# A graph network kernel: inverse roots of the last node updates by GpSimd's pow, and both passes without their last step

## The reference, cut to what matters

```python
h = relu(layernorm(x))
hn = mlp_node(h); he = mlp_edge(edge_attr)                      # 64 wide
msgs = mlp_msg(concat(hn[dst], hn[src], he))                    # 200,000 x 64
agg = segment_sum(msgs, dst) / max(counts, 1)
o = h + mlp_upd(concat(h, agg))
x = x + layernorm(o) * ln_g + ln_b                              # layer 1

h = relu(layernorm(x))
hw = h @ W                                                      # 4 heads of 32
e = leaky_relu(a_src[src] + a_dst[dst])                         # with a loop per node
p = exp(e - segment_max(e, dst))
x = x + segment_sum(hw[src] * p, dst) / segment_sum(p, dst) + bias   # layer 2
```

## Time and profile before

| | us |
|---|---|
| median of 3 runs | 4091.20 |
| lowest and highest | 4089.45, 4092.23 |
| the profiled execution, its own time | 4091.22 |
| its span, from the first to the last instruction | 4089.1 |
| busy: PE, DVE, ACT, POOL | 3382.9, 2517.0, 2850.5, 2965.8 |
| mean granted clock of TensorE | 0.838 of full speed |

### The profile page before, as it was taken

The page is one execution under the profiler, slowest core; times in us unless marked ns, Lnnn a source line. Parts: engine busy times, 40 slices in busy tenths (PEclk is TensorE's granted clock), DMA queues, the critical chain, the costliest instruction groups (busy, mean ns, idle before and its releaser), DMA issues. The chain is left out here.

```text
span 4089.1 us, 126775 instructions
## 1 busy us (share of the span) xinstructions
PE 3382.9 (83%) x30848; PEld 2976.2 (73%) x30849; DVE 2517.0 (62%) x10511; ACT 2850.5 (70%) x5940; POOL 2965.8 (73%) x3134
## 2 busy tenths in 40 slices
PE   7789888999988899999947777777777778777777
PEld 4677777777777788888847777777777767766776
DVE  5752222222222256777748777777777777888888
ACT  6466565656556577788738777777777777877777
POOL 2677777777777777777737777777777777777774
PEclk8789999999899899999967777777777777777777
DMA  5322222222222233333342222222222222332332
GB/s 159 88 60 53 54 55 53 56 53 53 55 54 53 60 83 91 91 96 95 81 120 58 57 58 58 57 58 58 58 57 58 58 58 63 79 78 76 78 78 58
DMA packets 319769, 282.90 MB, mean 69 GB/s; under 512 B 143418, under 2 KB 242924, under 8 KB 319532
## 3 DMA queue, kind: packets, MB, share of 16 engines
q0 software_dynamic: 99456, 159.33, 15.9%
q1 hardware_dynamic: 139224, 79.62, 7.4%
q10 hardware_dynamic: 80852, 41.75, 3.5%
HBM read 249.58 MB, written 29.40 MB: 68 GB/s over the span
## 5 line engine op out<-in xcount | busy, mean ns | idle before, releaser
L541 POOL DMA_INDIRECT a_G<-Htab,idx x1554 | 1470.8, 946 | 526.3 <-issue 464.0
L541 POOL DMA_INDIRECT p_rows<-Btab,idx x1554 | 1471.4, 947 | 475.1 <-issue 473.4
L1799 PE MATMUL a_psA<-a_GP,a_S 128*128 128x132 f32 x4704 | 892.5, 365 | 2.7 <-DVE a_GP L1634 2.7
L1799 PEld LDWEIGHTS a_psA<-a_GP,a_S 128*128 128x128 f32 x4704 | 821.5, 268 | 8.2 <-DVE a_GP L1634 3.1
L1056 DVE TENSOR_TENSOR p_z<-p_psZ,p_rows 128x512 f32<-128x512 f32 x294 | 195.9, 689 | 829.4 <-SPq L746 679.6
L1206 ACT COPY p_ST<-p_psT 128x1024 bf16<-128x1024 bf16 x294 | 300.5, 1022 | 563.7 <-PE p_psT L1318 543.4
L1730 ACT CAST a_S<-a_Sb 128x512 f32<-128x512 bf16 x588 | 608.6, 1144 | 0.0
L1365 PE MATMUL p_psA<-p_msg,p_S 128*128 128x65 f32 x4704 | 589.9, 284 | 10.9 <-ACT p_S L1227 9.8
L1365 PEld LDWEIGHTS p_psA<-p_msg,p_S 128*128 128x128 f32 x4704 | 571.6, 201 | 16.5 <-issue 12.8
L1227 ACT CAST p_S<-p_Sb 128x1024 f32 (+1 forms) x294 | 582.6, 1982 | 0.0
L1341 PEld LDWEIGHTS p_psZ<-wc,p_s 128*128 128x128 f32 x2352 | 325.1, 206 | 204.7 <-issue 103.5
(11 more groups left out here) (212 smaller groups left out, 5165.8 us busy)
## 6 DMA issues: line engine op xcount, KB each, us to landing
arena<-in_ea SPq DMA_DIRECT2D x196, 256.0 KB
p_single<-Btab SPq DMA_DIRECT2D x1792, 0.2 KB
a_single<-Htab SPq DMA_DIRECT2D x1792, 0.5 KB
p_rows<-Btab,idx POOLq DMA_INDIRECT x1554
a_G<-Htab,idx POOLq DMA_INDIRECT x1554
Htab<-u_H ACTq DMA_DIRECT2D x49, 136.0 KB
arena<-Htab SPq DMA_DIRECT2D x7, 952.0 KB
n_x<-in_x SPq DMA_DIRECT2D x14, 448.0 KB, 4.0
```

The costliest lines, as they stand in the source:

```text
L541: pool.indirect_dma_start(out=rows[:, u * C + c, :], out_offset=None, in_=table, in_offset=bass.IndirectOffsetOnAxis(ap=idx[u][:, c:c + 1] ...
L1799: m = pe.matmul(psA[v][:, 0:HR], S32[v][:, c, :], GP[v][:, c, :], start=c == 0, stop=c == C - 1)
```

## The change

Two parts. First, the number of steps that both passes run is NJ = NS - 1 = 293 instead of 294: step 293 is left out on every engine, in both passes; the tables keep their size. Second, in rows 148 to 152 of the first pass (LATE = 148 to SECOND + NQ - 1), which come when GpSimd has no gathers left, VectorE's ten instructions of guess and Newton steps are replaced by one `tensor_tensor` with `pow` on GpSimd, by a tile `minus` of -0.5 that GpSimd fills at the start of the pass. VectorE makes `ve`, then `u_xb` (which stood in `update_out` before the statistics), and waits for GpSimd's root. The counts of `s_root` go on by 2 a row instead of 11.

```diff
+NJ = NS - 1
...
+LATE = 148
...
     def edge(j, back):
-        return 0 <= j - back < NS
+        return 0 <= j - back < NJ
...
 def run_steps(eng, body, depth):
-    run_pairs(eng, body, NS, depth)
+    run_pairs(eng, body, NJ, depth)
...
     def valid(j):
-        return 0 <= j < NS
+        return 0 <= j < NJ
...
-    ve, root, square, shift = (sb(f"u_{n}", [P, 2, 2]) for n in ("ve", "root", "square", "shift"))
+    ve, root, square, shift, minus = (sb(f"u_{n}", [P, 2, 2]) for n in ("ve", "root", "square", "shift", "minus"))
...
+            pool.memset(minus[:, :, :], -0.5).then_inc(s_i, 1)
             gather_blocks(nc, pool, Btab, rows, idx, s_z, s_turn, k, 0, s_table)
+            pool.wait_ge(s_i, 4)
+            for row in range(LATE, SECOND + NQ):
+                ready = LINKS * (LATE - NORM) + 2 * (row - LATE) + 1
+                pool.wait_ge(s_root, ready)
+                pool.tensor_tensor(root[:, :, :], ve[:, :, :], minus[:, :, :], ALU.pow).then_inc(s_root, 1)
...
+            def update_xb(q):
+                dve.tensor_tensor(xb[:, :, :], xq[:, bass.ds(q % RQ, 1)].rearrange("p o w f -> p (o w) f"),
+                                  bc(k["lnb"][:, :], 1, 2), ALU.add).then_inc(s_xb, 1)
+
-            def update_out(q):
+            def update_out(q, late):
...
-                dve.tensor_tensor(xb[:, :, :], xq[:, bass.ds(q % RQ, 1)].rearrange("p o w f -> p (o w) f"),
-                                  bc(k["lnb"][:, :], 1, 2), ALU.add).then_inc(s_xb, 1)
+                if not late:
+                    update_xb(q)
...
+                if isinstance(row, int) and row >= LATE:
+                    late = LINKS * (LATE - NORM) + 2 * (row - LATE)
+                    dve.tensor_scalar(ve[:, :, :], mv[:, :, :, 1], LN_EPS, None, ALU.add).then_inc(s_root, 1)
+                    if first is not None:
+                        update_xb(first)
+                    dve.wait_ge(s_root, late + 2)
+                    return
                 dve.tensor_scalar(ve[:, :, :], mv[:, :, :, 1], LN_EPS, None, ALU.add).then_inc(s_root, 1)
...
-                    done = min(at_agg + 2, NS) if isinstance(row, int) else at_agg + 2
+                    done = min(at_agg + 2, NJ) if isinstance(row, int) else at_agg + 2
...
                 if up(row - NORM):
-                    update_out(row - NORM)
+                    update_out(row - NORM, isinstance(row, int) and row >= LATE)
...
-                summed = min(2 * row - 5, NS) if isinstance(row, int) else 2 * row - 5
+                summed = min(2 * row - 5, NJ) if isinstance(row, int) else 2 * row - 5
...
     def valid(j, back):
-        return 0 <= j - back < NS
+        return 0 <= j - back < NJ
```

## The result

| | before | after |
|---|---|---|
| median, beside each other | 4091.07 (4086.40 to 4099.93, 20 runs) | 4084.60 (4075.67 to 4091.82, 20 runs) |
| the profiled execution, its own time | 4091.22 | 4080.93 |
| its span | 4089.1 | 4079.2 |
| mean granted clock of TensorE | 0.838 | 0.833 |

The ratio of after to before is 0.9981, with a 95% interval of 0.9975 to 0.9987: 7.7 us faster, between 5.3 and 10.2. The predicted time was 4082.2.

What follows compares the result with a forecast made beforehand. GpSimd's gathers were taken to set the middle of both passes, leaving savings only in two tails: first -3.4 - 0.1 - 0.5 = -4.0 us, second -5.0, together -9.0, so 4091.2 became 4082.2 us; range 4078.5 to 4087.5.

Steps and rivals of the forecast that it cites:

- faster by over 0.2%: Whole kernel: a time below 4083.0 us, more than 8.2 us under the kernel before; chance 0.57.
- case "same": Whole kernel: a change within about 0.2% (8.2 us), which a measurement can't tell from none; chance 0.40.
- Second tail: Drain after the second pass's last gathers, rows 145 to 148: step 293's work and waits go, -5.0 us.
- Roots: First tail, late rows: pow replaces VectorE's Newton chain, but ScalarE's and TensorE's 4.5 us cycle stays; -0.1 us.
- Rival 3: Late rows of the first pass: pow after 1554 gathers costs far more; at 8 us, about 4102 us; chance 0.03.
- The step in the first tail: Rows 147 to 149: without step 293's matmuls and sum, mean_T(48)'s copy comes right behind relu_x1(45); -3.4 us.
- The psZ matmuls of step 293 in this row: TensorE, row 148 of the first tail: they only fill a wait for ScalarE, so removing them gives nothing.
- Clock: First tail: TensorE's clock fall may come at another moment; -0.5 us, bounds +1.0 and -1.2.
- The middle of both passes is set by GpSimd: Both passes between their tails: GpSimd's gathers set the pace, so other engines' savings there don't shorten the run.
- a gap of 48 to 50 us between the passes: Sign of being right: GpSimd's gap from last to next pass's first gather shrinks to this from 52.8 us.
- Rivals 1 and 4: First tail gives about -0.5 us, total 4085.7 (chance 0.15); step was free, within 1 us of before (chance 0.02).
- Rival 2: TensorE's clock stays high through row 149 and in the last sums: 4080.7 us; chance 0.12.

Runs made afterwards that it cites:

- g3_first_pass: g0_after with the empty step 293 kept in the second pass, left out in the first only: 4089.17 us against 4080.55, ratio 0.9992 to the kernel before.
- g0_after: Control: the changed kernel with only the block-end table in 16 bits and numbers floored at 0 in a register: 4080.55 us, ratio 0.9966 to the kernel before.
- e1_step_only: e0_after_u16 with step 293 left out but the Newton chain kept in rows 148 to 152, without GpSimd's pow: 4108.95 us against 4109.27.
- f5_pow_twice: f0_after with the inverse roots made twice on GpSimd in each of the five late rows: 4104.20 us against 4103.22.
- g7_stores_sp: g0_after with SyncE instead of ScalarE issuing the stores of heads and x1 from row 148 on: 4072.82 us, ratio 0.9953 to the kernel before.
- e0_after_u16: Control: the changed kernel with its tables of blocks and windows as 16-bit instead of 32-bit integers: 4109.27 us, ratio 1.0034 to the kernel before.
- f0_after: Control: the changed kernel with 16-bit block numbers for the waits, VectorE's second-pass table kept at 32 bits: 4103.22 us, ratio 1.0022 to the kernel before.

## Why the prediction was right, and where it was not

Time and range held: 4084.6 us measured, 4082.2 forecast, 4078.5 to 4087.5 the range. The chances leaned to faster by over 0.2% (0.57); by the ratio it is 0.19%, so the case "same" (0.40) came in by a hair. By its steps:

- **Second tail, -5.0: right.** -5.19 in the changed kernel, -5.44 by the step alone (g3_first_pass against g0_after). L1428 is on the chain where it was said to be.
- **Roots, -0.1: right.** e1_step_only shows 0 and f5_pow_twice why: ScalarE's row of 4.55 us covers VectorE's. The price of the pow was set too high, 1.6 us from ve to shift against the 1.29 to 1.44 measured, 1.01 to 1.11 of it the pow, and nothing hung on it. Rival 3, a pow of over 7 us after 1554 gathers, fell: the first one takes 1.07 us. The Trainium skill (GPSIMD Engine Reference, section Instruction dispatch) lets a freshly loaded kernel's first call cost some 6 us more. The trace shows no such cost at either first call, 1.52 us in the opening and 1.07 us after the gathers; whether the kernel was loaded afresh at either, no run shows.
- **The step in the first tail, -3.4: right in its mechanism, too small.** u_aT(48) comes right behind relu_x1(45), and the removed sum (3.52 us) gave only the 2.0 us of the table's third part. But ahead of it the prediction had -1.5, and the table has 32.84, 32.34 and 31.78 against 29.45 to 29.62: -2.8 in the mean, -3.2 in the profiled pair. The step that failed is "The psZ matmuls of step 293 in this row only fill a wait for ScalarE, I cost them at nothing": they cost 1.09 us. What they filled was a wait, but an instruction of another queue, the store, stood behind the matmuls after them. That leaves 1.7 us of the mean for the work of row 147, forecast at 1.5 and not tried alone, and for the time between ScalarE's two stores. The spread with the step in is mostly that time, 2.96, 2.58 and 1.98 us with the same code; the prediction took this as one fixed transfer.
- **Clock, -0.5: not confirmed.** In the profiled pair the sum of step 292 took 0.31 us more than before, and over all executions it lies anywhere from 1.97 to 3.65 us. The bounds, +1.0 and -1.2, were about right.
- **"The middle of both passes is set by GpSimd": wrong for the first pass.** From about row 110 on its rows go at TensorE's pace (97% busy in a row, 5.5 us of waiting for gathers in 250). So the expected sign, a gap of 48 to 50 us between the passes, failed (52.9), though the tail got 4.9 us shorter. It changed nothing in the sum, as no work of those rows was touched.
- **Rivals 1 and 4** (0.5 us in the first tail; the step free) fell by the tails. Rival 2 (the clock stays high through row 149) was not seen in this kernel: e1_step_only and g3_first_pass run the sum at 2.4 GHz (1.97 us), but there the clock falls right behind it. Only g7_stores_sp keeps it 4.8 us longer.

One thing stays open. The tails give 10.1 us in the profiled pair and 4.9 + 5.4 by the control pairs; whole times give 7.7 (5.3 to 10.2) for the changed kernel and 13.9 (8.6 to 19.2) for g0_after. That agrees only at the edges. From the first gather to the last `rel` the three executions that keep the step in the first pass took 1927.9 to 1930.9 us, the eleven without it 1929.4 to 1938.1, though the instructions of those rows are the same. It may be the chance of the slow rows or something that the shorter program does to them; 14 executions don't settle it.

## What to carry to other kernels

Measure a tail from an instruction that both kernels share and that sits on the path, not from the last instruction of the busiest engine: that engine may only be early. An instruction that fills a wait isn't free until what stands behind it in every queue has been followed, and a DMA issue behind a wait for another engine is the first place to look. Where a chain alternates between engines, removing work from the one that is not late (the roots) gives nothing; moving two DMA issues a row off the one that is late shortened the first tail by 4.9 us more against g3_first_pass, as much as the step gave there, a part of it by the clock.

## What the runs showed of the hardware

- Reading 14 numbers of 16 bits into registers cost VectorE some 1.9 us more than 14 of 32 bits (e0_after_u16 against the changed kernel). ScalarE's idle time ahead of a_ST grew by 1.5 us a read with 14 of 16 bits (e0_after_u16), and by 1.8 us with seven of 16 and seven of 32 in two loads (f0_after). A floor by a register operation ahead of the wait cost nothing that shows in g0_after.
- The clock of TensorE can fall for part of one row in a stretch where its load has not changed (1849.5 to 1864.5 above), which makes the row 1.7 us longer. It came back by the next row, whose psH takes 1.12 us again, and in five executions such rows stand five rows apart.
- `pow` on GpSimd for 128x4 values takes 1.01 to 1.11 us, with VectorE waiting 0.90 to 1.12 us for it.
- ScalarE's queue issued a store 0.1 us after TensorE's matmuls that an earlier ScalarE instruction waits for, and up to 0.9 us before that instruction started (g0_after).
